# Score products of two self-attentions spread between the passes of the unit that follows

## The reference

```python
x = _layernorm(x + _L0_attn_ref(x, wq, wk, wv, wo))      # 32 query heads, 8 key/value heads, head size 128
q, k, v = x @ wq.T, x @ wk.T, x @ wv.T
s = einsum('bhgnd,bhmd->bhgnm', q, k) * scale            # 64 x 64 scores of each head of each sequence
p = softmax(where(mask, s, -inf)); o = einsum('bhgnm,bhmd->bhgnd', p, v)
return o @ wo.T
...
x = _layernorm(x + _L1_attn_ref(x, w_qkv, w_o))          # the same sizes, a bias by distance in place of the window
```

## Time and profile before

| what | value |
|---|---|
| median of three runs | 2286.74 us (2285.29 to 2286.99) |
| the profiled execution, its own time | 2280.18 us |
| its span, first to last instruction | 2278.4 us |
| PE busy | 2171.6 us, 95% |
| PEld busy | 1757.2 us, 77% |
| DVE busy | 1300.4 us, 57% |
| POOL busy | 788.0 us, 35% |
| ACT busy | 741.2 us, 33% |

### The profile page before, as it was taken

The page is one execution under the profiler, slowest core; times in us unless marked ns, Lnnn a source line. Parts: engine busy times, 40 slices in busy tenths (PEclk is TensorE's granted clock), DMA queues, the critical chain, the costliest instruction groups (busy, mean ns, idle before and its releaser), DMA issues.

```text
span 2278.4 us, 34224 instructions
## 1 busy us (share of the span) xinstructions
PE 2171.6 (95%) x11954; PEld 1757.2 (77%) x11954; DVE 1300.4 (57%) x2158; ACT 741.2 (33%) x1428; POOL 788.0 (35%) x723
## 2 busy tenths in 40 slices
PE   8999999998999889998999999999989999999978
PEld 6888888886566567886788888887778888888867
DVE  3454454447889723344454455445686777766765
ACT  2232322233777612222322233222233233333321
POOL 4221222212455455354222222220453434434233
PEclk9999999999999989999999999999999999999999
DMA  4213222212000304211322212321222212222120
GB/s 169 71 60 83 83 54 65 83 29 75 19 20 18 114 23 146 92 55 57 85 53 70 78 55 81 84 61 47 66 70 70 69 47 78 69 69 60 30 77 38
DMA packets 120547, 152.43 MB, mean 67 GB/s; under 512 B 16272, under 2 KB 67984, under 8 KB 119952
## 3 DMA queue, kind: packets, MB, share of 16 engines
q1 hardware_dynamic: 120464, 151.33, 22.9%
HBM read 124.02 MB, written 27.26 MB: 66 GB/s over the span
## 4 chain that ended last, share of the span: by engine, by line
PE 78%; issue 8%; DVE 7%; POOL 5%; ACT 1%; DMA 1%; POOLq 0%; DVEq 0%; ACTq 0%; SPq 0%
PE banks L282 20%; PE banks L284 19%; PE banks L283 19%; PE banks L597 7%; PE banks L640 3%; POOL f_wl L1697 2%; PE banks L1244 1%; PE banks L1251 1%; PE banks L1214 1%; PE banks L1261 1%; PE banks L1280 1%; PE banks L1230 1%; POOL f_il L1705 1%; DVE st L350 1%; DVE X L935 1%
## 5 line engine op out<-in xcount | busy, mean ns | idle before, releaser
L282 PE MATMUL banks<-xTh,wh 128*128 128x512 f32 x1024 | 418.0, 408 | 11.5 <-DVE xTl L1972 7.4
L284 PE MATMUL banks<-xTh,wl 128*128 128x512 f32 x1024 | 404.1, 395 | 0.0
L283 PE MATMUL banks<-xTl,wh 128*128 128x512 f32 x1024 | 403.0, 394 | 0.0
L282 PE MATMUL banks<-woh,oth 128*128 128x512 f32 x768 | 313.3, 408 | 16.2 <-DVE X L935 7.0
L283 PE MATMUL banks<-wol,oth 128*128 128x512 f32 x768 | 301.7, 393 | 0.0
L284 PE MATMUL banks<-woh,otl 128*128 128x512 f32 x768 | 301.5, 393 | 0.0
L1030 POOL TENSOR_TENSOR sc_sb<-sc_sb,rs 128x512 f32<-128x512 f32 x96 | 103.9, 1086 | 551.5 <-DVE rs L889 551.5
L935 DVE TENSOR_TENSOR X<-banks,X 128x512 f32<-128x512 f32 x192 | 132.0, 687 | 271.8 <-PE banks L284 271.0
L732 ACT ACTIVATE q_sb<-banks 128x512 f32<-128x512 f32 x192 | 114.6, 597 | 400.5 <-PE banks L284 400.5
L282 PEld LDWEIGHTS banks<-xTh,wh 128*128 128x128 f32 x1024 | 195.1, 191 | 53.0 <-issue 9.2
L284 PEld LDWEIGHTS banks<-xTh,wl 128*128 128x128 f32 x1024 | 194.5, 190 | 43.5
(11 more groups left out here) (212 smaller groups left out, 3920.6 us busy)
## 6 DMA issues: line engine op xcount, KB each, us to landing
raw<-in_a_in SPq DMA_DIRECT2D x144, 256.0 KB, 2.9
raw<-in_a_out SPq DMA_DIRECT2D x96, 256.0 KB, 2.8
turned<-pq SPq DMA_DIRECT2D x384, 64.0 KB, 1.8
pt<-turned SPq DMA_DIRECT2D x96, 256.0 KB, 2.8
f_q<-in_f_q SPq DMA_DIRECT2D x21, 512.0 KB, 3.8
f_s<-in_f_s SPq DMA_DIRECT2D x21, 512.0 KB, 5.1
X<-in_x SPq DMA_DIRECT2D x1, 2048.0 KB, 10.6
x_craw<-in_ctx SPq DMA_DIRECT2D x8, 256.0 KB, 2.7
```

Of the source, the lines that this page charges most:

```text
L282: nc.tensor.matmul(out, w_hi, x_hi, start=start, stop=False)
L283: nc.tensor.matmul(out, w_hi, x_lo, start=False, stop=False)
L284: return nc.tensor.matmul(out, w_lo, x_hi, start=False, stop=stop)
```

## The change

`mm3` takes an iterator `between` and advances it after each of its passes, save the last pass of a unit. `scores` still makes its waits at its old place, but gives back a generator; its eight products are issued one at a time, whenever a pass of the projection unit or of the output product that follows has been issued. What is left when another kind of step comes is issued at once, and in `xattn1` all is issued at once. No computation is added or removed.

```diff
@@ -276,12 +276,17 @@
         def f32(ap):
             return ap.bitcast(F32)
 
-        def mm3(out, w, x, start, stop):
+        def mm3(out, w, x, start, stop, between=iter(())):
 
             (w_hi, w_lo), (x_hi, x_lo) = w, x
             nc.tensor.matmul(out, w_hi, x_hi, start=start, stop=False)
+            next(between, None)
             nc.tensor.matmul(out, w_hi, x_lo, start=False, stop=False)
-            return nc.tensor.matmul(out, w_lo, x_hi, start=False, stop=stop)
+            next(between, None)
+            last = nc.tensor.matmul(out, w_lo, x_hi, start=False, stop=stop)
+            if not stop:
+                next(between, None)
+            return last
 
         def xtile(t):
             return X[:, t * DM:(t + 1) * DM] if isinstance(t, int) else X[:, bass.ds(t * DM, DM)]
@@ -558,7 +563,7 @@
                 move_in(NKV - 1, pair)
 
 
-        def pe_unit(pe, st, i, u):
+        def pe_unit(pe, st, i, u, between=iter(())):
             kind, g, n = st.units[u]
             c = st.chunk_of(u)
             if n == 0:
@@ -574,14 +579,14 @@
                 for k in range(KT):
                     if st.name == "attn0" and isinstance(i, int) and u < 2 and k % 2 == 0:
                         pe.wait_ge(x0_ready, 2 * u + k // 2 + 1)
-                    last = mm3(bank[:, :], w(k), (xTh[:, k, cols], xTl[:, k, cols]), k == 0, k == KT - 1)
+                    last = mm3(bank[:, :], w(k), (xTh[:, k, cols], xTl[:, k, cols]), k == 0, k == KT - 1, between)
             else:
                 for m in range(2):
                     t = 2 * n + m
                     for k in range(KT):
                         last = mm3(bank[:, 2 * m * HD:2 * (m + 1) * HD],
                                    (cTh[:, k, t * P:(t + 1) * P], cTl[:, k, t * P:(t + 1) * P]),
-                                   (wh[:, 0:2, k, :], wl[:, 0:2, k, :]), k == 0, k == KT - 1)
+                                   (wh[:, 0:2, k, :], wl[:, 0:2, k, :]), k == 0, k == KT - 1, between)
             last.then_inc(A["proj_done"], 1)
 
         def pe_attention(pe, st):
@@ -591,13 +596,18 @@
                 if st.rms:
                     st.need(pe, "kt_ready", 2 * i + 2)
                 st.need(pe, "s_out", 4 * i + pair)
+                return score_products(i, pair)
+
+            def score_products(i, pair):
                 for c in range(2):
                     for m in range(4):
                         col = pair * 2 * P + m * S
                         last = nc.tensor.matmul(pb[2][:, (4 * c + m) * S:(4 * c + m + 1) * S],
                                                 q_sb[:, 4 * (pair % 2) + m, c * P:(c + 1) * P], k_sb[:, col:col + S],
                                                 start=True, stop=True)
-                last.then_inc(A["sc_done"], 1)
+                        if (c, m) == (1, 3):
+                            last.then_inc(A["sc_done"], 1)
+                        yield
 
             def square_sums(i, j):
                 st.need(pe, "sq_sum", 4 * i + j + 1)
@@ -641,7 +651,7 @@
                                                     start=v_part is vh and p_part == 0, stop=v_part is vl)
                 last.then_inc(A["pv_done"], 1)
 
-            def project_out(i, t, tail):
+            def project_out(i, t, tail, between=iter(())):
                 st.need(pe, "o_ready", 8 * i + 2 * (t // 2) + 2)
                 st.need(pe, "x_added", 8 * i + t - 1 if tail and t else 8 * i + t)
                 if tail and t == 1:
@@ -652,17 +662,28 @@
                         st.need(pe, "wo_ready", 4 * i + g + 1)
                     rows = 4 * (t % 2) + g
                     last = mm3(bank[:, :], (oth[:, t // 2 % 2, rows, :], otl[:, t // 2 % 2, rows, :]),
-                               (woh[:, g, :], wol[:, g, :]), g == 0, g == G - 1)
+                               (woh[:, g, :], wol[:, g, :]), g == 0, g == G - 1, between)
                 last.then_inc(A["wo_done"], 1)
 
             def run(i, events, tail=False):
+                between = iter(())
                 for kind, n, age in events:
                     j = i - age
+                    if kind not in ("U_", "WO", "SC"):
+                        for _ in between:
+                            pass
                     if kind == "U_":
                         if not (st.name == "xattn1" and isinstance(j, int) and j == 0 and n < 2):
-                            pe_unit(pe, st, j, n)
+                            pe_unit(pe, st, j, n, between)
+                            for _ in between:
+                                pass
                     elif kind == "SC":
-                        scores(j, n)
+                        for _ in between:
+                            pass
+                        between = scores(j, n)
+                        if st.rms:
+                            for _ in between:
+                                pass
                     elif kind == "SS":
                         square_sums(j, n)
                     elif kind == "KT":
@@ -672,7 +693,11 @@
                     elif kind == "PV":
                         probs_v(j, n)
                     elif kind == "WO":
-                        project_out(j, n, tail and age == 1)
+                        project_out(j, n, tail and age == 1, between)
+                        for _ in between:
+                            pass
+                for _ in between:
+                    pass
 
             if st.name == "attn1":
                 pe.wait_ge(const_set, 2)
```

## The result

| | median | runs |
|---|---|---|
| before | 2282.42 us | 20 |
| changed | 2285.63 us | 20 |

The ratio is 1.0015, with an interval of 1.0008 to 1.0022: slower by 3.4 us, between 1.8 and 5.0. One of the changed kernel's 20 runs took 5385.78 us and is left out of the ratio. With 20 runs the kernel before has a median 4 us under that of the three runs that stood ahead of the prediction. The forecast was +7.0 us, more than twice the measured rise, and of its two terms only the wait of couple 3 is among what the 3.4 us consist of.

What follows compares the result with a forecast made beforehand. The prediction took TensorE, busy 95% of the span, to bound the kernel. Spread products +3.8, couple 3's wait +3.2 and the transpose of v 0 gave +7.0 us on 2286.74: 2293.7 us, range 2285 to 2299.5.

Steps and rivals of the forecast that it cites:

- the wait of couple 3: Couple 3, right behind U_10, must wait until VectorE has read couple 2: TensorE stalls 0.20 us in 16 groups, +3.2 us.
- What bounds: TensorE, busy 423.46 of 423.80 us in six groups of the first self-attention; changes to its row move the end one for one.
- How many move: In attn0 and attn1 couples 1, 2 and 3 go into U_6, U_10 and U_11; couple 0 stays a row: 48 couples, 384 products.
- No load is hidden: Only one weight load runs ahead on TensorE, so 16 loads a couple are paid, in a row or spread out.
- Rival B: Both loads of a spread product hide under long passes: 32 us back less some 5, 2260 us; chance 0.07.
- The price of a spread product: Between two passes a product costs 0.24 us, as in xattn1; 1.92 against 1.85 a couple, +3.8 us over 48 couples.
- The low end: For the spread products' price: a product costs 0.224 us as in a row and the tail of slow passes vanishes, -2.7 us.
- The sign named for it: New entry in TensorE's waits: the units' first pass on L875 of VectorE, 16 times, about 0.2 to 0.7 us as displayed.
- Weights, transfers, SyncE: nothing.: The unit's waits w_ready and proj_free come 1.8 us sooner, but all they ask for is older: no cost.
- In chains whose end is wanted in the next group: ScalarE and GpSimd get couples 1 to 3 up to 2 us later, in chains ending at PT: no cost.
- The transpose of v: Behind U_11, vl comes 0.14 us late, covered by TensorE's own delay and a load's lead: 0, at most 2.4 us.
- rival A: Even exchange: spread products cost what a row costs, couple 3's wait mostly hidden under the load's lead; about 2289 us, chance 0.19.

## Why the prediction was wrong

- *What bounds.* Right in the main: the terms below, added one for one, give the measured time within its interval. But "423.46 of 423.80 busy" did not mean that nothing waits. A record of 0.39 us reaches over the next start at 0.23, so a wait of 0.1 or 0.2 us leaves no idle time behind; only starts against starts show it, and WO0 at 3.2 us instead of 2.8 would have.
- *How many move.* Right, 48 couples, couple 0 in a row.
- *No load is hidden.* Right: two open loads a product, 0.226 us. Rival B, the gain, came out at nothing.
- *The price of a spread product, +3.8 us.* Wrong in size: 0.5 us at most (0.04 us a group for the tail). The step that failed is the choice of the lone product's 0.24 over the row's 0.224, when the same two open loads had just been counted in both. The low end (-2.7; its own numbers give -2.8) had been worked from the row, but took the tail away too.
- *The wait of couple 3, +3.2 us.* Right in place and kind, sized 0.20 where 0.135 was measured: 2.2 us. VectorE started 0.08 us earlier than forecast, because the products cost less, and the release took 0.05 us to the load. The sign named for it, an entry in TensorE's waits 16 times, could not appear: the wait leaves no idle time in the matmuls. The waits of the weight loads have it, over the whole trace as `PEld banks L282 <- DVE sc_sb L900: 3.0, 10, 0.3`.
- *"Weights, transfers, SyncE: nothing."* The step that failed worst. I had looked at TensorE's waits for weights, and not at who else waits for `s_out`: SyncE does, for the bias of attn1, with chunk 5's load queued behind. 0.46 us in seven groups, 3.2 us. "In chains whose end is wanted in the next group" was true of the probabilities, and false of the splits that stand behind them in VectorE's row. The wait for these splits was in the trace of before already, 0.36 to 0.38 us in each WO0, and I had not looked for it.
- *The transpose of v.* Right: no wait on `vl` appears.
- *The first group's clock.* Not in the prediction. The late fall met 7 of 10 stages with rows and costs 1.5 us, so a gain of 1 us a stage on average, 2 in all.

Together 0.5 + 2.2 + 3.2 - 2.0 = 3.9 us, against 3.4 measured (1.8 to 5.0). The time lies in the range by luck as much as by reason: the three runs behind it stood 4 us too high, and the errors of the terms cancel in part. The rise is nearest to rival A's (2.3 us), but not by A's reason: the exchange was even, as A says, the wait was not hidden, and a loss that I had missed and a gain that I had missed stood against each other.

## What to carry to other kernels

Count the loads that stay open before spreading small products between large ones: where each small record needs its own weights and only one load runs ahead, mixing moves the hidden load about and gains nothing. When a semaphore comes later, list all who wait for it, the transfer queues too, with what is queued behind each of them. In a kernel whose busiest engine has no slack, look for its small regular waits: here 0.37 us at fourteen places was worth 3.9 us, as much as the change cost. Such waits show in starts against starts and in the waits of the weight loads, not in the idle time of the matmuls.

## What the runs showed of the hardware

- The columns that a short float32 record moves were free up to 128: rows of records with 64 and with 128 columns took the same 1.701 us a couple, 0.112 us from record to record, each with a load of 128 x 128 weights.
- Met waits on semaphores ahead of short products and passes cost TensorE nothing in the steady groups (1.701 and 4.587 us with and without); behind couple 0 of a first group, where TensorE waits for VectorE, the next pass came 0.15 us later with them.
- TensorE's granted clock fell from 2.4 to 1.2 GHz after idle times of only 0.7 and 1.0 us around rows of short records. With two such rows it fell in 10 of 10 stages profiled, in 7 of them behind the second row and in 3 ahead of it; with the second row mixed between long passes it never fell behind it, and ahead of it in 6 of 18. What decides whether it falls early is open.
- Two VectorE subtractions that began together with a GpSimd subtraction took 2.35 us, and 1.30 us where GpSimd was idle. That it is the two sharing something was not tested by itself.
